# Local attention: row sums behind the row maxima, the token shift in four parts, the output product behind the weighted values

## The chip, the cores and the metric

The kernel runs on one core of one Trainium2 chip. The metric is the device time of one execution in microseconds (us). Three executions of the kernel before took 1742.20, 1739.64 and 1736.16 us, a median of 1739.64.

## The reference

The program computes four blocks with residuals over 16 x 256 tokens of 128 features: a linear attention with two decays, a mixture of eight experts, a retention layer, and a two-layer local attention with a gated feed-forward network. The change is in the attention half of the last block, which runs twice (DEPTH is 2). Its core, for each layer:

```python
h = shift_token(x)                  # features 64..127 come from the token before
qkv = h @ wqkv                      # 8 heads of 64
q = l2norm(q) * qs                  # row sums of squares, then 1/sqrt
k = l2norm(k) * ksc
q, k = rotary_xpos(q, k)
...
sim = jnp.einsum('bhwid,bhwjd->bhwij', bq, bk)      # windows of 64, one back
sim = jnp.where(mask, -jnp.finfo(sim.dtype).max, sim)
attn = jax.nn.softmax(sim, axis=-1)                 # subtracts the row maximum
out = jnp.einsum('bhwij,bhwjd->bhwid', attn, bv)
...
x = x + o @ wo
```

## The kernel before, in words

`local_layer(k, l, shared)` does one layer. The 4096 tokens are 8 chunks of 512 columns (two sequences of 256); a chunk has 4 tiles of 128 tokens (`t`), and 8 pairs of units (`p`: a pair is two heads of one sequence). Every engine runs the same software pipeline, written out by hand: `steps` calls `step` ten times. In step g the chunk g is projected (`project`), the scores and weighted values of chunk g-1 are made (`attend`), and what is left of chunk g-2 is finished (`finish`). Step 0 of a layer only projects, step 1 projects and attends, steps 2 to 7 do all three (they are the body of a loop of two steps), steps 8 and 9 drain. A step has 8 blocks (`blk`). Tile t belongs to blocks 2t and 2t+1. Semaphores join the engines; on each engine the order is the order of the code.

In an even block PE (TensorE) runs `project_qk` (six matmuls, L1582, into the PSUM banks BA and BB); ACT squares both banks (`squares`, L1733); DVE multiplies both with the rotation table (`rotate`, L1836), sums the squares by head (`lengths`, L1843 and the clip L1846); ACT turns the sums into 1/sqrt (`norms`, L1738 and L1741); POOL adds the two rotated halves (L1557) and multiplies with the norms (L1564). In an odd block PE runs `project_v` (L1591) once the first half of the rotation has read bank BA, ACT copies it (`keep_values`, L1762), and PE transposes the tile before (`turn`, L1608), which ACT copies twice (`keep_rows`, L1749 and L1756). The next `project_qk` waits for the L1749 copies.

Beside that, every block of a full step carries attention work on pairs, each stage a block or more behind the last: `maxima_scores` on PE (L1622, L1626), `maxima` on DVE (L1855, L1857: the masked row maxima, `nm`), `scores` and `less_maxima` on PE (L1643 to L1658), `weights` on ACT (L1773, exp), `weighted_values` on PE (L1670, L1671), `denominators` on ACT (L1779, L1781), `normalise` on DVE (L1866). The maxima use two PSUM banks for every pair, so `maxima_scores` of a block waits until DVE has read the maxima of the block before:

```python
need(pe, max_r, NU * c + 2 * p)
```

In blocks 2 and 6 the maxima of half a chunk are also transposed by PE (L1677) and copied by ACT (`maxima_rows`, L1767), and `less_maxima` waits for that copy. In block 4 of a finishing step PE runs `output` (L1687, eight matmul records), which needs bank BB and therefore the whole rotation of the tile; DVE adds it in block 5 (`add_output`, L1873). The token shift of the next chunk (`shift_chunk`, L1819 to L1823: the rounded value `hs_hi` and the rest `hs_lo`, halves of 64 partitions each) runs on DVE at the end of block 6, and the first `project_qk` of the next step waits for it (`shifted`).

Of the kernel before, what the change touches and what calls it, by code (L numbers as in the profile page):

```python
# [15 lines left out]
P = 128  # L16
# [1426 lines left out]
def later(a):  # L1443

    return a.rearrange("p (s t) -> p s t", t=SEQ)[:, :, 1:SEQ]
# [19 lines left out]
def need(eng, sem, value):  # L1465

    if not isinstance(value, int) or value > 0:
        eng.wait_ge(sem, value)


def local_layer(k, l, shared):
# [5 lines left out]
    with ExitStack() as big:  # L1477
# [4 lines left out]
        with ExitStack() as ctx:  # L1482
# [86 lines left out]
            def _(pe):  # L1569
# [120 lines left out]
                def step(g, par, project, attend, finish):  # L1690
                    now = (g, par, project, attend, finish)
                    for blk in range(2 * NTILE):
# [17 lines left out]
                            less_maxima(sc[0], sc[2])  # L1710
                        if blk % 2 and rows:
                            turn(rows[0], rows[2], project, g - 2 if finish and blk == 5 else None)
                        if finish and blk == 4:
                            output(g - 2, par, NTILE * g + t if project else None)
                        if mx and blk in (2, 6):
                            maxima_scores(*mx)
                        if av:
                            weighted_values(*av)

                steps(pe, step)  # L1720

            @block.scalar
            def _(act):
# [59 lines left out]
                def step(g, par, project, attend, finish):  # L1783
                    now = (g, par, project, attend, finish)
                    for blk in range(2 * NTILE):
                        t = blk // 2
                        if project and blk % 2 == 0:
                            squares(g, t)
                        if project and blk % 2:
                            keep_values(g, par, t)  # L1790
                        rows = turned_at(g, par, project, attend, blk)
                        if attend and blk in (2, 6):
                            maxima_rows(g - 1, blk // 4)
                        dn = staged(*now, blk, 4)
                        if dn:
                            denominators(dn[0], dn[2])
                        sc = staged(*now, blk, 2)
                        if sc:
                            weights(sc[0], sc[2])
                        if blk % 2 and rows:  # L1800
                            keep_rows(*rows)
                        if project and blk % 2 == 0:
                            norms(g, t)

                steps(act, step)
# [2 lines left out]
            def _(dve):  # L1808
# [3 lines left out]
                        nc.vector.tensor_scalar(t[:], k.H[:, T:T + CH], 1.0, None, ALU.mult).then_inc(made, 1)  # L1812
                dve.wait_ge(made, 5 * L)

                def shift_chunk(g, par):

                    hi, lo = hs[0][par], hs[1][par]
                    early_rows, late_rows = shifted_views(k, here(g))
                    nc.vector.tensor_scalar(hi[0:DH, :], early_rows, 1.0, None, ALU.mult)  # L1819
                    nc.vector.tensor_scalar(later(hi[DH:P, :]), late_rows, 1.0, None, ALU.mult).then_inc(hs_hi, 1)  # L1820
                    dve.wait_ge(hs_hi, g + 1 + l)
                    nc.vector.tensor_tensor(lo[0:DH, :], early_rows, hi[0:DH, :].bitcast(F32), ALU.subtract)
                    nc.vector.tensor_tensor(later(lo[DH:P, :]), late_rows, later(hi[DH:P, :]).bitcast(F32),  # L1823
                                            ALU.subtract).then_inc(shifted, 1)

                shift_chunk(G0, 0)
                dve.wait_ge(zeroed, 4 * L)

                def rotate(g, t):
# [54 lines left out]
                def step(g, par, project, attend, finish):  # L1884
                    now = (g, par, project, attend, finish)
                    for blk in range(2 * NTILE):
                        t = blk // 2
                        if project and blk % 2 == 0:
                            rotate(g, t)
                            lengths(g, t)  # L1890
                        if finish and blk == 5:
                            add_output(g - 2)
                        mx = maxima_at(g, project, attend, blk)
# [4 lines left out]
                        nr = staged(*now, blk, 4)  # L1898
                        if nr:
                            normalise(*nr)  # L1900
                        if project and blk == 6:
                            need(dve, v_mm, NTILE * g)
                            shift_chunk(g + 1, 1 - par)

                steps(dve, step)

# [239 lines left out]
```

## Time and profile before

| what | value |
|---|---|
| runs of the kernel before, us | 1742.20, 1739.64, 1736.16 |
| the profiled execution's own time, us | 1738.83 |
| its span, us | 1737.0 |
| busy in the span | PE 1400.4 (81%), DVE 1153.1 (66%), ACT 939.0 (54%), POOL 620.9 (36%) |
| the two attention stages, us from the span's start | 740.6 to about 1124, 1239.7 to about 1625 |

The span is the profiled execution from its first instruction to its last; the 1.8 us around it belong to the time too. A group line reads: line, engine, operation, names of what is written and read, number of instructions, then busy time and mean duration in ns, then the idle time of the engine just before them and what ended most of it. PE counts matmuls, PEld weight loads.

### The profile page before, as it was taken

Reading aid. Unit: us, or ns where it says so; the run is one execution under the profiler, and the core shown is the slowest. Engines: PE = TensorE matmul, PEld = TensorE weight load, DVE = VectorE, ACT = ScalarE, POOL = GpSimd, SP = SyncE. Lnnn points to the kernel's source line nnn. Section 1 sums busy time; section 2 is a strip of 40 time slices with the busy share of each in tenths; the row PEclk is TensorE's granted clock in tenths of the full one; section 3 lists DMA queues with packets and bytes.
Section 4 is the critical chain, followed back from the end, with each engine's and each line's share of the span. In section 5 each row is a group of like instructions: output and inputs, shape, how many; then the busy total and the mean of one; then the engine's idle time right before and its main releaser. Section 6 shows DMA issues by size and latency. Waiting matters only on the chain. (4 is left out here: it accounts for less than half of the span.)

```text
span 1737.0 us, 24232 instructions
## 1 busy us (share of the span) xinstructions
PE 1400.4 (81%) x7076; PEld 889.5 (51%) x7076; DVE 1153.1 (66%) x2595; ACT 939.0 (54%) x1756; POOL 620.9 (36%) x536
## 2 busy tenths in 40 slices
PE   6799998656399667668888988988578889889887
PEld 3233333444388532146666666733356666666433
DVE  1499999387288654457777777544568777776343
ACT  5523332443266335636777777644257777776543
POOL 0244343357366630344444434020344434442000
PEclk9899999678699979859999999999669999999998
DMA  4500000311212130000000000000000000000001
GB/s 132 195 1 1 0 1 1 87 48 50 71 60 81 37 133 0 19 1 1 2 2 0 1 1 1 1 26 0 19 1 2 2 1 0 1 0 1 1 0 49
DMA packets 35305, 44.53 MB, mean 26 GB/s; under 512 B 5652, under 2 KB 25137, under 8 KB 35200
## 3 DMA queue, kind: packets, MB, share of 16 engines
q1 hardware_dynamic: 30592, 34.91, 6.4%
q0 software_dynamic: 4608, 8.47, 1.5%
q8 instruction: 36, 0.59, 0.1%
q14 instruction: 69, 0.57, 0.1%
HBM read 23.28 MB, written 21.12 MB: 26 GB/s over the span
## 5 line engine op out<-in xcount | busy, mean ns | idle before, releaser
L1557 POOL TENSOR_TENSOR R<-R 128x512 f32<-128x512 f32 x128 | 159.3, 1265 | 392.9 <-DVE R L1836 392.9
L1836 DVE TENSOR_TENSOR R<-bank,tab 128x1024 f32<-128x1024 f32 x128 | 151.7, 1220 | 137.9 <-ACT sq L1733 132.7
L1564 POOL TENSOR_TENSOR R<-R,rn 128x512 f32<-128x512 f32 x128 | 133.7, 1065 | 12.1 <-issue 10.0
L1670 PE MATMUL bank<-PT,VA 128*128 128x192 f32 x512 | 131.4, 339 | 0.0
L1866 DVE TENSOR_TENSOR OT<-bank,rd 64x256 f32<-64x256 f32 x256 | 106.2, 415 | 18.2 <-ACT rd L1781 16.5
L1733 ACT ACTIVATE sq<-bank 128x512 f32<-128x512 f32 x128 | 76.2, 597 | 64.6 <-PE bank L1582 58.6
L1773 ACT ACTIVATE PT<-bank 128x320 f32<-128x320 f32 x256 | 98.3, 435 | 16.0 <-PE bank L1658 11.2
L1195 POOL DMA_INDIRECT expert_rows<-Yt,xin x80 | 82.5, 1031 | 67.7 <-DVE Yt L1168 49.7
L1582 PE MATMUL bank<-wqkv_hi,hs_hi 128*128 128x512 f32 x128 | 63.1, 493 | 49.3 <-DVE hs_lo L1823 39.3
L1855 DVE CUSTOM_DVE_ANT_0 masked<-bank,mask_q 128x128 bf16<-128x128 f32 x256 | 73.7, 288 | 42.0 <-PE bank L1626 31.4
L617 DVE TENSOR_TENSOR_SCAN S<-beta,U 128x512 f32<-128x512 f32 x64 | 100.0, 1583 | 0.0
L1671 PE MATMUL bank<-PT,VA 128*128 128x128 f32 x512 | 99.0, 275 | 0.0
L1671 PEld LDWEIGHTS bank<-PT,VA 128*128 128x128 f32 x512 | 91.3, 192 | 0.0
L1622 PE MATMUL bank<-QKr 64*128 64x128 f32 x256 | 42.9, 332 | 59.6 <-DVE nm L1857 59.6
L1857 DVE CUSTOM_DVE_ANT_0 masked<-bank,mask_q 128x192 bf16<-128x192 f32 x256 | 90.2, 352 | 0.2 <-issue 0.2
L1779 ACT ACTIVATE rd<-bank 64x512 f32<-64x512 f32 x128 | 76.0, 593 | 16.7 <-PE bank L1671 14.1
L1670 PEld LDWEIGHTS bank<-PT,VA 128*128 128x128 f32 x512 | 79.5, 193 | 9.5 <-issue 6.7
L1781 ACT ACTIVATE rd<-rd 64x512 f32<-64x512 f32 x128 | 80.7, 631 | 4.1
L1608 PE MATMUL bank<-ident,R 128*128 128x128 f32 x512 | 76.2, 296 | 6.0 <-ACT VA L1762 5.7
L1749 ACT ACTIVATE QK<-bank 128x512 f32<-128x512 f32 x128 | 71.0, 608 | 11.9 <-PE bank L1608 11.8
L1843 DVE TENSOR_REDUCE ss<-sq 128x16 f32<-128x1024 f32 x64 | 77.3, 1208 | 0.0
L888 POOL DMA_INDIRECT expert_slots<-tok_rows,dst x64 | 64.1, 1001 | 33.6 <-issue 18.0
(311 smaller groups left out, 3805.6 us busy)
## 6 DMA issues: line engine op xcount, KB each, us to landing
expert_slots<-empty SPq DMA_DIRECT2D x8, 650.0 KB, 6.5
xin<-expert_slots SPq DMA_DIRECT2D x8, 650.0 KB, 5.1
expert_rows<-empty SPq DMA_DIRECT2D x8, 512.0 KB, 6.7
pair_rows<-expert_rows SPq DMA_DIRECT2D x16, 256.0 KB, 3.8
expert_raw<-w1e_dram SPq DMA_DIRECT2D x9, 256.0 KB, 2.9
expert_raw<-w2e_dram SPq DMA_DIRECT2D x9, 256.0 KB, 2.9
tok<-x_dram SPq DMA_DIRECT2D x8, 256.0 KB, 4.8
out_dram<-tok_out SPq DMA_DIRECT2D x8, 256.0 KB, 2.5
```

What stands on the lines that cost most here:

```text
L617: nc.vector.tensor_tensor_scan(S[i][:], beta[i % 2][:, chunk(c)], U[i // 2][:], 0.0, ALU.mult, ALU.add).then_inc(s_scan, 1)
L1195: nc.gpsimd.indirect_dma_start(k.ys[:, :], bass.IndirectOffsetOnAxis(ap=ids, axis=0), Yt[:, s % 3, t, :], None, bounds_check=2 * T - 1, oo ...
L1557: nc.gpsimd.tensor_tensor(halves[:, :, 0, :, z, :], halves[:, :, 0, :, z, :], halves[:, :, 1, :, 1 - z, :], ALU.add).then_inc(summed, 1)
L1564: nc.gpsimd.tensor_tensor(x, x, scale.to_broadcast([P, HEADS, DH]), ALU.mult).then_inc(normed, 1)
L1670: nc.tensor.matmul(bank[:, o:o + KW], VA[par][:, 2 * s, h, :], pt[:, 0:KW], start=True, stop=True)
L1671: nc.tensor.matmul(bank[:, o + P:o + SEQ], VA[par][:, 2 * s + 1, h, :], pt[:, KW:KW + P], start=False, stop=True, skip_group_check=True).t ...
L1773: nc.scalar.activation(PT[:, u % 4, :], ps[BT + u % 2][:, 0:KW + P], ACT.Exp, scale=QK_SCALE).then_inc(pt_r, 1)
L1781: nc.scalar.activation(rd[:, p % 2, :], rd[:, p % 2, :], ACT.Exp, scale=-1.0).then_inc(rd_r, 1)
L1836: nc.vector.tensor_tensor(R[:, i, qk, :, :].rearrange("p c (h d) -> p c h d", d=DH), x, y.to_broadcast([P, 2, HEADS, DH]), ALU.mult).then_ ...
L1843: nc.vector.tensor_reduce(ss[:, i, :], sq[:].rearrange("p q (h d) -> p (q h) d", d=DH), AX.X, ALU.add).then_inc(sums_r, 1)
L1857: nc.vector.tensor_tensor_reduce(masked[:, v % 2, KW:2 * KW], bank[:, KW:2 * KW], mask[:, KW:2 * KW], -1.0, FAR, ALU.add, ALU.min, nm[:, 2 ...
L1866: m = nc.vector.tensor_tensor(OT[par][i * DH:(i + 1) * DH, b, s * SEQ:(s + 1) * SEQ], ps[BO + p % 2][0:DH, i * SEQ:(i + 1) * SEQ], rd[:, p ...
```

## The change

Nothing is computed in another way, and no instruction is added or removed: instructions move on three engines.

- DVE: `lengths` moves from just behind `rotate` to the end of the even block, behind `maxima` and `normalise`. `shift_chunk` is cut into its four instructions, and one of them ends each odd block (part 0 in block 1, part 3 in block 7).
- ACT: in odd blocks `denominators` stands first, ahead of `keep_values`; `norms` moves from the end of the even block to the end of the odd block, behind `keep_rows`.
- PE: in block 4 `output` runs behind `weighted_values`.

```diff
                         if blk % 2 and rows:
                             turn(rows[0], rows[2], project, g - 2 if finish and blk == 5 else None)
-                        if finish and blk == 4:
-                            output(g - 2, par, NTILE * g + t if project else None)
                         if mx and blk in (2, 6):
                             maxima_scores(*mx)
                         if av:
                             weighted_values(*av)
+                        if finish and blk == 4:
+                            output(g - 2, par, NTILE * g + t if project else None)
...
                         if project and blk % 2 == 0:
                             squares(g, t)
+                        dn = staged(*now, blk, 4)
+                        if dn and blk % 2:
+                            denominators(dn[0], dn[2])
                         if project and blk % 2:
                             keep_values(g, par, t)
                         rows = turned_at(g, par, project, attend, blk)
                         if attend and blk in (2, 6):
                             maxima_rows(g - 1, blk // 4)
-                        dn = staged(*now, blk, 4)
-                        if dn:
+                        if dn and blk % 2 == 0:
                             denominators(dn[0], dn[2])
                         sc = staged(*now, blk, 2)
                         if sc:
                             weights(sc[0], sc[2])
                         if blk % 2 and rows:
                             keep_rows(*rows)
-                        if project and blk % 2 == 0:
+                        if project and blk % 2:
                             norms(g, t)
...
-                def shift_chunk(g, par):
+                def shift_part(g, par, part):
...
-                    nc.vector.tensor_scalar(hi[0:DH, :], early_rows, 1.0, None, ALU.mult)
-                    nc.vector.tensor_scalar(later(hi[DH:P, :]), late_rows, 1.0, None, ALU.mult).then_inc(hs_hi, 1)
-                    dve.wait_ge(hs_hi, g + 1 + l)
-                    nc.vector.tensor_tensor(lo[0:DH, :], early_rows, hi[0:DH, :].bitcast(F32), ALU.subtract)
-                    nc.vector.tensor_tensor(later(lo[DH:P, :]), late_rows, later(hi[DH:P, :]).bitcast(F32),
-                                            ALU.subtract).then_inc(shifted, 1)
...
+                    if part == 0:
+                        need(dve, v_mm, NTILE * (g - 1))
+                        nc.vector.tensor_scalar(hi[0:DH, :], early_rows, 1.0, None, ALU.mult)
+                    elif part == 1:
+                        nc.vector.tensor_scalar(later(hi[DH:P, :]), late_rows, 1.0, None, ALU.mult).then_inc(hs_hi, 1)
+                    elif part == 2:
+                        dve.wait_ge(hs_hi, g + 1 + l)
+                        nc.vector.tensor_tensor(lo[0:DH, :], early_rows, hi[0:DH, :].bitcast(F32), ALU.subtract)
+                    else:
+                        nc.vector.tensor_tensor(later(lo[DH:P, :]), late_rows, later(hi[DH:P, :]).bitcast(F32),
+                                                ALU.subtract).then_inc(shifted, 1)
...
                         if project and blk % 2 == 0:
                             rotate(g, t)
-                            lengths(g, t)
                         if finish and blk == 5:
                             add_output(g - 2)
                         mx = maxima_at(g, project, attend, blk)
...
                         if nr:
                             normalise(*nr)
-                        if project and blk == 6:
-                            need(dve, v_mm, NTILE * g)
-                            shift_chunk(g + 1, 1 - par)
+                        if project and blk % 2 == 0:
+                            lengths(g, t)
+                        if project and blk % 2:
+                            shift_part(g + 1, 1 - par, t)
```

DVE in an even block of step 1, before; each `masked,nm` row with the `nm` row behind it is one of the maxima of a pair.

```order
L1836 TENSOR_TENSOR R<-bank,tab 128x1024 x2
L1843 TENSOR_REDUCE ss<-sq 128x16
L1846 TENSOR_SCALAR ss<-ss 128x16
L1855 ISA masked,nm<-bank,mask_q 128x128
L1855 ISA nm 128x1
L1857 ISA masked,nm<-bank,mask_q 128x192
L1857 ISA nm 128x1
L1855 ISA masked,nm<-bank,mask_q 128x128
L1855 ISA nm 128x1
L1857 ISA masked,nm<-bank,mask_q 128x192
L1857 ISA nm 128x1
```

The same place now (lines are numbered anew: L1844 is the rotation, L1863 and L1865 the maxima, L1851 and L1854 the row sums and their clip).

```order
L1844 TENSOR_TENSOR R<-bank,tab 128x1024 x2
L1863 ISA masked,nm<-bank,mask_q 128x128
L1863 ISA nm 128x1
L1865 ISA masked,nm<-bank,mask_q 128x192
L1865 ISA nm 128x1
L1863 ISA masked,nm<-bank,mask_q 128x128
L1863 ISA nm 128x1
L1865 ISA masked,nm<-bank,mask_q 128x192
L1865 ISA nm 128x1
L1851 TENSOR_REDUCE ss<-sq 128x16
L1854 TENSOR_SCALAR ss<-ss 128x16
```

The maxima follow the rotation directly, and the two instructions of the row sums stand behind them.

ACT in blocks 4 and 5 of step 1, before; `sq` is the squares, `rd` the denominators, `PT` the weights, `ss` and `rn` the norms, `VA` the values, `QK` and `QKr` the kept rows.

```order
L1733 ACTIVATE sq<-bank 128x512 x2
L1779 ACTIVATE rd<-bank 64x512
L1781 ACTIVATE rd<-rd 64x512
L1773 ACTIVATE PT<-bank 128x320 x2
L1738 ACTIVATE ss<-ss 128x16
L1741 ACTIVATE rn<-ss,lnb 128x16
L1762 ACTIVATE VA_1<-bank 128x8x64
L1779 ACTIVATE rd<-bank 64x512
L1781 ACTIVATE rd<-rd 64x512
L1773 ACTIVATE PT<-bank 128x320 x2
L1749 ACTIVATE QK_1<-bank 128x4x128 x2
L1756 ACTIVATE QKr<-QK_1 128x4x128 x2
```

And now:

```order
L1733 ACTIVATE sq<-bank 128x512 x2
L1779 ACTIVATE rd<-bank 64x512
L1781 ACTIVATE rd<-rd 64x512
L1773 ACTIVATE PT<-bank 128x320 x2
L1779 ACTIVATE rd<-bank 64x512
L1781 ACTIVATE rd<-rd 64x512
L1762 ACTIVATE VA_1<-bank 128x8x64
L1773 ACTIVATE PT<-bank 128x320 x2
L1749 ACTIVATE QK_1<-bank 128x4x128 x2
L1756 ACTIVATE QKr<-QK_1 128x4x128 x2
L1738 ACTIVATE ss<-ss 128x16
L1741 ACTIVATE rn<-ss,lnb 128x16
```

The norms stand between the kept rows and the squares of the next tile; the second pair of `rd` is ahead of `VA`.

PE at the end of block 4 of a full step, as a piece of the difference (`OT` goes through the output product, `PT` through the weighted values; L1589 belongs to the `project_v` of block 5).

```order
 L1658 MATMUL bank<-mT_0,sel 128x128
+L1670 MATMUL bank<-PT,VA_1 128x192
+L1671 MATMUL bank<-PT,VA_1 128x128
+L1670 MATMUL bank<-PT,VA_1 128x192
+L1671 MATMUL bank<-PT,VA_1 128x128
 L1681 REGISTER_ALU
 L1687 MATMUL bank<-OT_0,wo_0 128x512 x4
-L1670 MATMUL bank<-PT,VA_1 128x192
-L1671 MATMUL bank<-PT,VA_1 128x128
-L1670 MATMUL bank<-PT,VA_1 128x192
-L1671 MATMUL bank<-PT,VA_1 128x128
 L1589 REGISTER_ALU
```

The output product changes places with the weighted values of the block.

## Rows read from the trace of the kernel before

**Rows 1.** Windows of step 0 and of full steps in the first layer; columns named above.
```profile
core 0: us, PE busy (x) PEld busy (x) DVE busy (x) ACT busy (x) POOL busy (x), PEclk, DMA share, GB/s
740.60:777.70 37.10, 23.91 (x69) 15.24 (x69) 20.11 (x29) 15.04 (x32) 18.25 (x16) 0.59 0.00 1
821.00:1078.00 257.00, 226.49 (x1731) 173.97 (x1730) 194.72 (x602) 189.19 (x400) 105.19 (x92) 0.99 0.00 1
```

**Rows 2.** Waits of the whole span: us in total, times, longest.
```profile
ACT ss L1738 <- DVE ss L1846: 89.0, 64, 2.8
...
PE bank L1622 <- DVE nm L1857: 59.6, 48, 2.7
...
PE bank L1582 <- DVE hs_lo L1823: 39.3, 16, 14.5
```

**Rows 3.** Windows of the four tiles of one full step, columns as rows 1.
```profile
1453.50:1463.30 9.80, 8.59 (x73) 6.99 (x74) 9.58 (x36) 7.24 (x16) 4.55 (x4) 1.00 0.00 0
1463.30:1473.10 9.80, 9.02 (x78) 7.22 (x76) 7.50 (x25) 8.34 (x19) 4.54 (x4) 1.00 0.00 0
1473.10:1486.40 13.30, 12.41 (x83) 8.62 (x82) 8.38 (x27) 8.24 (x18) 4.54 (x4) 1.00 0.00 1
1486.40:1497.30 10.90, 9.21 (x74) 7.24 (x74) 8.82 (x19) 9.40 (x21) 4.72 (x4) 1.00 0.00 0
```

**Rows 4.** Timeline of PE over that step: start, us, instruction, idle before it.
```profile
1453.54 0.50 PE L1582 MATMUL bank<-wqkv_hi,hs_hi 128*128 128x512 f32 x1 [0.83 <-DVE hs_lo L1823]
...
1460.15 0.33 PE L1622 MATMUL bank<-QKr 64*128 64x128 f32 x2 [1.16 <-DVE nm L1857]
...
1465.98 0.23 PE L1656 MATMUL bank<-mT,sel 128*128 128x128 bf16 x1
...
1466.76 0.59 PE L1670 MATMUL bank<-PT,VA 128*128 128x192 f32 x2
...
1467.88 0.48 PE L1591 MATMUL bank<-wqkv_hi,hs_hi 128*128 128x512 f32 x1
...
1469.90 0.33 PE L1622 MATMUL bank<-QKr 64*128 64x128 f32 x2 [0.78 <-DVE nm L1857]
...
1477.22 3.70 PE L1687 MATMUL bank<-OT,wo 128*128 128x512 f32 x8 [0.83 <-DVE R L1836]
...
1493.17 0.33 PE L1622 MATMUL bank<-QKr 64*128 64x128 f32 x2 [0.90 <-DVE nm L1857]
```

**Rows 5.** Timeline of ACT, start of its second tile.
```profile
1463.08 1.17 ACT L1756 ACTIVATE QKr<-QK 128x512 fp32r<-128x512 f32 x2
1464.29 1.30 ACT L1733 ACTIVATE sq<-bank 128x512 f32<-128x512 f32 x2
1465.48 0.27 ACT L1767 ACTIVATE mT<-bank 128x128 bf16<-128x128 bf16 x1
```

**Rows 6.** Timeline of DVE, same tile.
```profile
1465.01 2.35 DVE L1836 TENSOR_TENSOR R<-bank,tab 128x1024 f32<-128x1024 f32 x2 [1.55 <-ACT sq L1733]
1467.28 1.21 DVE L1843 TENSOR_REDUCE ss<-sq 128x16 f32<-128x1024 f32 x1
1468.53 0.23 DVE L1846 TENSOR_SCALAR ss<-ss 128x16 f32<-128x16 f32 x1
...
1469.76 0.84 DVE L1866 TENSOR_TENSOR OT<-bank,rd 64x256 f32<-64x256 f32 x2
```

**Rows 7.** The shift: source view of L1819 (min/median/max), timelines of POOL and DVE.
```profile
L1819 DVE TENSOR_SCALAR hs_hi<-H x18: 418/722/880, 738.2 to 1583.1; 64x512 fp32r x12, 64x512 fp32r<-64x512 f32 x6
...
1493.31 2.23 POOL L1564 TENSOR_TENSOR R<-R,rn 128x512 f32<-128x512 f32 x2 [0.21 <-issue]
...
1494.65 1.17 DVE L1820 TENSOR_SCALAR hs_hi<-H 64x510 fp32r x1
```

**Rows 8.** Timelines of ACT and PE in step 0 of layer 0.
```profile
754.37 0.21 ACT L1738 ACTIVATE ss<-ss 128x16 f32<-128x16 f32 x1 [2.73 <-DVE ss L1846]
...
755.46 1.11 PE L1608 MATMUL bank<-ident,R 128*128 128x128 f32 x4 [1.29 <-ACT VA L1762]
```

**Rows 9.** Timeline of PE at the start of step 8, layer 0.
```profile
1090.48 0.33 PE L1622 MATMUL bank<-QKr 64*128 64x128 f32 x2 [1.54 <-DVE nm L1857]
```

More of the change, by code:

```diff
@@ L1813, in _ @@
                 dve.wait_ge(made, 5 * L)
-                def shift_chunk(g, par):
+                def shift_part(g, par, part):
                     hi, lo = hs[0][par], hs[1][par]
                     early_rows, late_rows = shifted_views(k, here(g))
-                    nc.vector.tensor_scalar(hi[0:DH, :], early_rows, 1.0, None, ALU.mult)
-                    nc.vector.tensor_scalar(later(hi[DH:P, :]), late_rows, 1.0, None, ALU.mult).then_inc(hs_hi, 1)
-                    dve.wait_ge(hs_hi, g + 1 + l)
-                    nc.vector.tensor_tensor(lo[0:DH, :], early_rows, hi[0:DH, :].bitcast(F32), ALU.subtract)
-                    nc.vector.tensor_tensor(later(lo[DH:P, :]), late_rows, later(hi[DH:P, :]).bitcast(F32),
-                                            ALU.subtract).then_inc(shifted, 1)
-                shift_chunk(G0, 0)
+                    if part == 0:
[9 more added lines that the diff above has]
+                                                ALU.subtract).then_inc(shifted, 1)
+                for part in range(4):
+                    shift_part(G0, 0, part)
                 dve.wait_ge(zeroed, 4 * L)
```

## The prediction

> **What bounds the kernel now.** First I read the windows of the two attention stages, since the change touches nothing else. In full steps PE is busy 226.5 of 257.0 us, DVE 194.7 and ACT 189.2, at a granted clock of 0.99 [rows 1]: PE is near its limit, and what can be won is its idle time. In step 0 PE is busy only 23.9 of 37.1 us, at a clock of 0.59 of full speed. Then I read the waits [rows 2]: PE waits 59.6 us in 48 waits, ahead of the matmuls for the maxima (L1622), for DVE's maxima of the block before; 39.3 us in 16 waits for the shifted tokens, of which one alone, at a layer's start, is 14.5. ACT waits 89.0 us in all 64 tiles for the clipped row sums. Last I read one full step on PE tile by tile [rows 3, 4]. Its tiles take 9.8, 9.8, 13.3 and 10.9, 43.8 us together. The waits are 1.16 in tile 0, 0.78 in tile 1, 0.83 before the output product in tile 2, and in tile 3 0.90 and, as the next projection starts, 0.83 as at the head of this one: 4.50 us a step that PE could gain at most. There are 12 such steps, 6 in each layer.
>
> **Row sums behind the maxima.** L1843 and L1846 take 1.21 + 0.23 us with small gaps, 1.44 to 1.5 together [rows 6]. They stand between the rotation and the maxima, for which PE waits in each odd block. Moved back, the maxima end 1.45 us earlier relative to the rotation's start. That covers the waits of 1.16, 0.78 and 0.90 if the rotation starts when it does now. All other terms ask whether it does, and what is late next.
>
> **Norms last on ACT.** In the kernel before, ACT stands idle in each even block until the clip is done. Now norms come after the kept rows, when the sums are long ready, so that wait goes. But the kept rows end at 1464.25 and the squares of the next tile start at 1464.29 [rows 5]: ACT is already late there, since PE's projection is ready by then. The two norms (0.21 for the first [rows 8]; with the second, slightly longer, and their gap about 0.55, an estimate) now sit in this place, on the path projection, squares, rotation. I take 0.55 us later for the squares and so for the rotation in tiles 1, 2 and 3 of a full step; least 0 (if denominators placed first let ACT reach the weights earlier; in tile 2 it does win about 0.35), at most 0.7. In blocks 2 and 6 the transposed maxima are copied behind the squares (L1767, ending 1465.75), and L1656, which waits for it, starts at 1465.98 [rows 4, 5]: 0.2 us of slack, so 0.35 to 0.5 turns into a new PE wait there in block 2.
>
> POOL's products come later with the norms, but their user, the transposition, is a block and a half further on; I cost that at nothing. If that cover failed, the transposes would wait up to POOL's 2.2 us [rows 7].
>
> **Full steps, tile by tile.**
> - Tile 0: the rotation follows a project_qk that itself waited for the shift, so ACT is free and the delay is hidden. The whole 1.16 goes. Saving 1.16 (0.8 to 1.16).
> - Tile 1: the 0.78 goes, but the new wait ahead of L1656 costs up to 0.5; behind it the maxima are in time. Saving 0.25. Bounds: 0.78, and a loss of 0.4 if part 0 of the shift is slow (below).
> - Tile 2: the output product waits 0.83 for the rotation. The weighted values, 1.12 us of PE work (1466.76 to 1467.88), now run inside that wait; against it stands the later rotation, 0.55, so that a wait of 0.2 to 0.5 is left. Saving 0.4 (0 to 0.83). DVE's add comes behind the product, as before, and DVE idles there.
> - Tile 3: the shift leaves block 6 (0.73 + 1.17 + 0.68 + 0.69, 3.3 us), but its last part, 0.69, stands in block 7 behind that block's maxima and normalise, and these behind the row sums. DVE's path, start to start [rows 6]: rotation 2.27, row sums 1.5, maxima 1.0, normalise 0.87. Before, from the rotation to the end of the shift: 2.27 + 1.5 + 1.0 + 0.87 + 3.35 = 9.0. Now: 2.27 + 1.0 + 0.87 + 1.5 + 1.0 + 0.87 + 0.69 = 8.2. Of the 0.8 won the later rotation takes about 0.4 back (0.55 less what the denominators win in tile 2). So this tile is still closed by the shift: the 0.90 wait goes, and the wait for hs_lo grows from 0.83 to about 1.3. Saving 0.4 (from -0.5 to 0.9).
>
> Together 1.16 + 0.25 + 0.4 + 0.4 = 2.21 a step, times 12 = 26.5 us.
>
> **The shift's parts.** The same instruction L1819 takes 0.418 at the least and 0.722 in the median; L1820 took 1.17 while POOL's second product ran [rows 7]. Part 0 now ends block 1: by the path above it starts some 1.2 us after the next projection (1.7 to the rotation, 8.0 behind it with the split of the maxima, less the tile's 8.6), and POOL's products of the tile, which wait for the norms, some 0.6 later. So it takes 0.42 or up to 1.17. The first is hidden by the wait for the squares, the second, if the order turns, delays the rotation of tile 1 by about 0.6: that is the loss bound of tile 1. I take the first; the other would take 0.65 x 12 = 8 us from the sum. The Trainium skill ("SBUF — State Buffer", section "SBUF: two separate sides") says that DVE in a two-port mode and GpSimd hold their shared port exclusively for a whole instruction; this trace agrees, as the 1.17 above beside 0.418 alone shows. By that rule spreading the parts puts some of them beside POOL's work and some not, and the slow part 0 would be the case of the sentence before.
>
> **Step 0, twice.** There ACT's values copy waits behind the norms, which wait 2.73 us for the sums; PE's second group of transposes waits 1.29 for that copy [rows 8], then the next projection for the kept rows. Now the copy runs as soon as project_v is done, about 1.4 earlier. I take 1.4 for tile 0, 1.2 each for tiles 1 and 2 (PE's first transposes fill the rest), and 1.4 for tile 3, where the row sums leave both the maxima's path and the shift's. 5.2 a layer, 10.4 in all (5 to 16: at the upper end a denser PE also gets its full clock sooner than at the 0.59 of now).
>
> **Step 1, twice.** Waits of up to 2.7 us for the maxima shrink by 1.1 in tiles 0 and 1 and 0.5 in tile 2, nothing in tile 3: 2.75 a layer, 5.5 in all (2 to 8).
>
> **End of step 7, twice.** No projection follows there, so the shift is only a burden: in the kernel before it held up the maxima of block 7 and PE waited 1.54 at the next maxima [rows 9], after 1.26 in the tile. Both go: 2.8 a layer, 5.6 in all (3 to 5.6). The drain in steps 8 and 9 has no projection and keeps its order but for the output product: 0.
>
> **Sum.** 26.5 + 10.4 + 5.5 + 5.6 = 48.0. The profiled execution took 1738.8 us (span 1737.0 and 1.8 around it), the median of the runs 1739.6, so the two differ by less than 1. I forecast 1739.6 - 48.0 = 1692 us.
>
> **Rivals.**
> 1. *Full steps give nothing* (chance 0.19). The waits turn up one for one at L1656, at L1687 and as a longer hs_lo wait, since ACT's squares and with them DVE's rotation are late in every tile. For it: ACT has no idle before the squares in three tiles of four [rows 5]. Against it: in tile 0 the squares are not held. Time: 1739.6 less the 21.5 of steps 0, 1 and 7 = 1718.
> 2. *More than the sum* (0.10). Denominators first bring ACT forward enough to hide the norms, tiles 1 to 3 lose 0.78, 0.83 and 0.9; with tile 0 that is 3.67 x 12 = 44, plus 21.5: 1674.
> 3. *Slower* (0.09). The loop closes through the last part of the shift. Place: project_qk of tile 0, waiting for hs_lo. Maxima, normalise and row sums all stand before part 3, and the rotation that starts the chain is itself later by the norms. If both of block 7's items wait for PE as well, the wait grows from 0.83 to over 5 us, a step loses 2.5 net; 12 x 2.5 = 30, less some 15 won in steps 0, 1 and 7: 1739.6 + 15 = 1755. It decides from where the hs_lo wait exceeds about 4.5 us; the chain above gives 1.3. Against it: DVE has 9.5 us of idle in a 43.8 us step (34.3 busy, the sum of [rows 3]).
> 4. *No change* (0.10): within 0.3%, which is about what a measurement of this kernel can tell from no change. PE's gaps are refilled everywhere, steps 0 and 1 included, as when PE loses in clock what it gains in waits. 1739.6.
>
> **How the numbers follow.** My forecast's own case has 0.52. Faster by over 0.3% (below 1734) are the forecast, rivals 1 and 2: 0.81; same 0.10; slower 0.09. The range reaches from 1680 (60 us: the upper bounds of most terms) to 1722 (rival 1, with some of its gains missing); it leaves out the last two rivals and part of the second.
>
> **What the profile of the changed kernel would show.** Right: the wait of PE's L1622 for the maxima falls from 59.6 us to under 15; ACT's wait for the clipped sums (89.0) vanishes; the hs_lo wait in full steps is 1 to 2 us each instead of 0.83; a new wait of some 0.4 at less_maxima (L1656) in block 2; the output product's wait is 0.2 to 0.5; a full step takes about 41.6 us instead of 43.8; step 0 takes 32 us instead of 37. Wrong: squares that start no later than now after the projection (then the step is shorter, near 40.5), or a step not shorter than 43.5 (rival 1), or an hs_lo wait beyond 3 us.

## The result and the profile after

The changed kernel took 1657.07 us in the median of four runs (1655.81 to 1662.76), against 1740.14 before: a ratio of 0.9524, with a 95% interval of 0.9503 to 0.9544. It is faster by 83 us, where I forecast 48 and a range down to 1680. The sign was right, and so was the main mechanism (the row sums no longer stand between the rotation and the maxima that PE waits for); the size was not.

The page of the profile after, its span and busy times; then the windows of step 0 and of full steps in layer 0, with the columns of [rows 1].

```profile
span 1656.2 us, 24233 instructions
PE 1384.4 (84%) x7076; PEld 879.5 (53%) x7076; DVE 1131.6 (68%) x2595; ACT 929.6 (56%) x1756; POOL 621.3 (38%) x536
```
```profile
739.90:767.60 27.70, 17.75 (x68) 11.13 (x68) 20.45 (x36) 14.59 (x31) 16.93 (x14) 0.81 0.00 1
804.90:1038.00 233.10, 224.30 (x1732) 172.38 (x1733) 187.28 (x602) 184.98 (x398) 104.96 (x92) 1.00 0.00 1
```

In full steps PE is now busy 96% of the time (224.3 of 233.1), before 88%. The waits of the whole span, as in [rows 2], lines numbered anew:

```profile
PE bank L1582 <- DVE hs_lo L1830: 44.9, 16, 14.5
...
PE bank L1622 <- DVE nm L1865: 4.2, 6, 1.1
...
PEld bank L1656 <- ACT mT L1767: 1.9, 6, 0.4
```

PE's wait for the maxima fell from 59.6 us to 4.2, ACT's 89.0 us for the clipped sums are gone from the list, and the wait for the shift grew from 39.3 to 44.9. The four tiles of the full step that was read before, now 1386.60 to 1426.75 (it answers to [rows 3]):

```profile
1386.60:1395.10 8.50, 8.50 (x73) 6.96 (x74) 6.60 (x23) 6.83 (x14) 4.56 (x4) 1.00 0.00 0
1395.10:1404.00 8.90, 8.90 (x77) 7.17 (x75) 8.12 (x28) 8.09 (x19) 4.57 (x4) 1.00 0.00 0
1404.00:1416.30 12.30, 12.23 (x83) 8.59 (x82) 9.56 (x31) 8.03 (x18) 4.54 (x4) 1.00 0.00 1
1416.30:1426.70 10.40, 9.18 (x77) 7.27 (x75) 8.48 (x26) 9.55 (x22) 4.55 (x4) 1.00 0.00 1
```

PE is busy without a gap in tiles 0 and 1, and but for 0.07 us in tile 2. Its timeline shows what is left; it answers to [rows 4]:

```profile
1386.60 0.50 PE L1582 MATMUL bank<-wqkv_hi,hs_hi 128*128 128x512 f32 x1 [1.26 <-DVE hs_lo L1830]
...
1397.79 0.23 PE L1656 MATMUL bank<-mT,sel 128*128 128x128 bf16 x1
...
1408.57 3.70 PE L1687 MATMUL bank<-OT,wo 128*128 128x512 f32 x8
...
1426.75 0.50 PE L1582 MATMUL bank<-wqkv_hi,hs_hi 128*128 128x512 f32 x1 [1.27 <-DVE hs_lo L1830]
```

Beside these 0.07 us there is one wait a step, 1.26 us for the last part of the shift. The following table cuts both profiled executions at the first matmul of the projections (L1582), and sets the difference beside the forecast's terms.

| stretch | before, us | after, us | gained | forecast |
|---|---|---|---|---|
| step 0, layers 0 and 1 | 37.1, 37.0 | 27.8, 30.9 | 15.4 | 10.4 |
| step 1 | 41.5, 41.8 | 37.3, 36.6 | 9.4 | 5.5 |
| steps 2 to 6 | 226.1, 224.2 | 204.1, 201.4 | 44.9 | 22.1 |
| step 7 to the next layer or the end | 194.5, 194.3 | 189.2, 189.1 | 10.4 | 10.0 |
| before the first projection | 740.6 | 739.9 | 0.8 | 0 |

Most of what I missed is in steps 2 to 6. A regular step fell from 43.86 to 40.16, tile by tile from 9.77, 9.79, 13.37, 10.94 to 8.53, 8.93, 12.30, 10.40. That is 3.70 us a step against my 2.21. Before, two steps of each layer were not regular: steps 4 and 6, each behind a jump of the loop (its body is two steps, so its jumps stand ahead of steps 4 and 6), took 47.6 and 45.7 us in layer 0, 47.2 and 45.4 in layer 1.

### The profile page after: what moved, and what is told of

The parts are those of the page before. It is cut to its first block and busy times, and to the rows that moved or that the text cites. A ratio compares the mean times of both kernels' runs of the same rounds, so it can differ in the third digit from the quotient of the medians.

```text
span 1656.2 us, 24233 instructions
## 1 busy us (share of the span) xinstructions
PE 1384.4 (84%) x7076; PEld 879.5 (53%) x7076; DVE 1131.6 (68%) x2595; ACT 929.6 (56%) x1756; POOL 621.3 (38%) x536
## 5 line engine op out<-in xcount | busy, mean ns | idle before, releaser
L1844 DVE TENSOR_TENSOR R<-bank,tab 128x1024 f32<-128x1024 f32 x128 | 151.5, 1221 | 93.9 <-ACT sq L1733 90.7
L1582 PE MATMUL bank<-wqkv_hi,hs_hi 128*128 128x512 f32 x128 | 61.3, 479 | 51.0 <-DVE hs_lo L1830 44.9
L1733 ACT ACTIVATE sq<-bank 128x512 f32<-128x512 f32 x128 | 71.0, 589 | 50.4 <-PE bank L1582 48.8
L1865 DVE CUSTOM_DVE_ANT_0 masked<-bank,mask_q 128x192 bf16<-128x192 f32 x256 | 90.4, 353 | 0.0
L1863 DVE CUSTOM_DVE_ANT_0 masked<-bank,mask_q 128x128 bf16<-128x128 f32 x256 | 73.5, 287 | 22.1 <-PE bank L1626 13.6
L1851 DVE TENSOR_REDUCE ss<-sq 128x16 f32<-128x1024 f32 x64 | 78.0, 1219 | 1.6
L1756 ACT ACTIVATE QKr<-QK 128x512 fp32r<-128x512 f32 x128 | 74.8, 649 | 0.0
L2010 DVE SCALAR_TENSOR_TENSOR Uf<-bank,vec,Gg 128x512 f32<-128x512 f32 (+1 forms) x48 | 36.0, 750 | 52.0 <-PE bank L1962 52.0
```

The costliest lines, as they stand in the source:

```text
L1844: nc.vector.tensor_tensor(R[:, i, qk, :, :].rearrange("p c (h d) -> p c h d", d=DH), x, y.to_broadcast([P, 2, HEADS, DH]), ALU.mult).then_ ...
L1851: nc.vector.tensor_reduce(ss[:, i, :], sq[:].rearrange("p q (h d) -> p (q h) d", d=DH), AX.X, ALU.add).then_inc(sums_r, 1)
L1865: nc.vector.tensor_tensor_reduce(masked[:, v % 2, KW:2 * KW], bank[:, KW:2 * KW], mask[:, KW:2 * KW], -1.0, FAR, ALU.add, ALU.min, nm[:, 2 ...
```

## The experiments

Twelve kernels ran. A ratio is always to the kernel before, run beside it on the same chip; on two of the chips everything outside the attention took some 30 to 50 us longer, for before too, so between chips I compare ratios and the lengths of regular steps; tiles that an edit leaves alone agree on all chips to some 0.01 us (8.53, 8.93 and 10.40 in u_output as in the changed kernel). "A step" is a regular full step in layer 1, from projection to projection: 43.86 us before, 40.16 after.

**Taking one edit back from the changed kernel.**

u_sums:
```diff
                             rotate(g, t)
+                            lengths(g, t)
...
-                        if project and blk % 2 == 0:
-                            lengths(g, t)
```


> The changed kernel with the row sums back between rotation and maxima; all else as changed (1657 us). Theory A (the row sums on the maxima's path are the main term, and the norms' later squares add to it, since the rotation now starts 0.35 us later): PE's waits for nm return, about 1.1 us in tile 0 and 1.1 in tile 1 of a full step, nothing in tile 3 (the shift closes that tile, and the chain to it holds the row sums either way): 2.2 x 12 = 27 us, and 3 to 4 us a layer in steps 0 and 1: about 1690. Theory B (the moves on ACT are what counts and the row sums' place is second): 1657 to 1668.

Measured: ratio 0.9815 (0.9775 to 0.9854), a step 42.77 us: tiles 9.83, 10.15, 12.28, 10.51. Theory A holds for the regular step: tiles 0 and 1 lose 1.3 and 1.2, tile 2 nothing and tile 3 0.1. The time that it gave, 1690 or a ratio of 0.971, was some 18 us too low: the steps behind the jumps of layer 0 take 47.2 and 47.8 us again (the changed kernel's 41.5 and 41.7), and steps 0 take 32.4 in both layers instead of 27.8 and 30.9. Its waits:
```profile
PE bank L1622 <- DVE nm L1865: 62.3, 45, 3.0
```

u_shift:
```diff
-                        if project and blk % 2:
-                            shift_part(g + 1, 1 - par, t)
+                        if project and blk == 6:
+                            for part in range(4):
+                                shift_part(g + 1, 1 - par, part)
```


> The changed kernel with all four parts of the shift at the end of block 6. Theory A (the spread shortens DVE's chain in tile 3 by some 0.7 us, and leaves DVE free 1.5 us earlier at the end of a step, which hides its restart after the loop's jump): full steps +0.7 to 1.0 us, the two jumps of each layer +1.5 us each, the end of step 7 +1.5 us a layer: about +18 us, 1675. Theory B (the spread only moves work that is hidden anyway): within 4 us of 1657.

Measured: 0.9511 (0.9475 to 0.9547), which can't be told from the changed kernel's. My theory A missed: a regular step is 40.10 us, as with the spread. The whole shift in block 6, on DVE's timeline:
```profile
874.93 0.42 DVE L1823 TENSOR_SCALAR hs_hi<-H 64x512 fp32r x1
875.37 0.42 DVE L1825 TENSOR_SCALAR hs_hi<-H 64x510 fp32r x1
```
In the kernel before, its first two parts took 0.72 (median) and 1.17 [rows 7], when they met POOL's products. With the norms late on ACT they come clear of them and take 0.42 each (in the full steps of o_act too, below), so the shift takes some 2.25 us instead of 3.3. Behind the jumps steps grow to 41.0 to 41.3; the stretch of steps 2 to 6 of both layers is 405.5 us, as in the changed kernel. With ACT's edit in place the spread is worth nothing that can be measured; alone (o_shift, below) it is worth 0.8 a step.

u_norms:
```diff
-                        if project and blk % 2:
+                        if project and blk % 2 == 0:
                             norms(g, t)
```


> The changed kernel with the norms back at the end of the even block, while the row sums stay behind maxima and normalise. Theory A (ACT's queue then waits for sums that are ready only some 7.3 us after the projection, and values copy, denominators, weights and kept rows queue behind): tiles 0 and 1 of a full step +2 to 3 us each, tile 3 +1.5, so +6 us x 12 = 70 and some 10 in steps 0 and 1: about 1735, all of the gain given back. Theory B (norms last costs 0.35 us of later squares and saves an ACT wait that nobody needed, so taking it back is neutral): 1650 to 1662.

Measured: 1.0284 (1.0240 to 1.0329), slower than before, a step 47.8 us in layer 1 and 50.9 in layer 0. Theory A holds and was too mild. Its longest wait:
```profile
ACT ss L1738 <- DVE ss L1854: 182.2, 64, 3.9
```

u_output:
```diff
+                        if finish and blk == 4:
+                            output(g - 2, par, NTILE * g + t if project else None)
                         if mx and blk in (2, 6):
                             maxima_scores(*mx)
                         if av:
                             weighted_values(*av)
-                        if finish and blk == 4:
-                            output(g - 2, par, NTILE * g + t if project else None)
```


> The changed kernel with the output product back ahead of the weighted values in block 4. Theory A (the wait for the rotation, now 0.07 us, comes back as 0.83 + 0.35 = 1.1 to 1.2, in 12 steps): +13 us, 1670. Theory B (what the product waits for comes late anyway, and the time is given back at the next wait): within 4 us of 1657.

Measured: 0.9567 (0.9527 to 0.9607). The step is 41.25 us, all of it in tile 2 (13.39 against 12.30): +1.09 a step, theory A. The interval overlaps with the changed kernel's, so it is the step that shows it, not the time.

**One edit alone on the kernel before.**

o_sums (the lines that u_sums takes back, put in alone):
```diff
                             rotate(g, t)
-                            lengths(g, t)
...
+                        if project and blk % 2 == 0:
+                            lengths(g, t)
```


> The kernel before (1740 us) with only the row sums moved behind maxima and normalise. Theory A (the moves need each other: ACT's norms, still at the end of the even block, now wait for sums that come 3 us later, and everything behind them on ACT is late): slower, 1775 to 1800. Theory B (PE's wait for the maxima goes, 1.16 + 0.78 + 0.90 a step): about 1705.

Measured: 1.0264 (1.0228 to 1.0301), 1787.9 us against 1743.1, a step 47.9. Theory A. PE's wait for the maxima does go, and ACT's takes its place:
```profile
ACT ss L1738 <- DVE ss L1846: 188.8, 64, 4.0
...
PE bank L1622 <- DVE nm L1857: 9.5, 10, 1.3
```

o_act:
```diff
+                        dn = staged(*now, blk, 4)
+                        if dn and blk % 2:
+                            denominators(dn[0], dn[2])
                         if project and blk % 2:
                             keep_values(g, par, t)
...
-                        dn = staged(*now, blk, 4)
-                        if dn:
+                        if dn and blk % 2 == 0:
                             denominators(dn[0], dn[2])
...
-                        if project and blk % 2 == 0:
+                        if project and blk % 2:
                             norms(g, t)
```


> The kernel before with only ACT's moves (norms last, denominators first in odd blocks). Theory A: steps 0 gain about 5 us a layer since the values copy no longer waits for the norms, full steps lose 0 to 0.35 us a tile because squares come later while the waits for the maxima stay: 1725 to 1735. Theory B (ACT's wait for the clipped sums, 89 us in all, was on the path): below 1710.

Measured: 0.9913 (0.9886 to 0.9941), 1728.0 us. A step is 43.9, unchanged, but its tiles are not: 10.11, 10.15, 13.39 and 10.23. Tiles 0 and 1 lose some 0.35 each, and tile 3 wins 0.7: the shift's first two parts take 0.42 each there, clear of POOL's products, and the wait for hs_lo is gone. Neither theory said that. Steps 0 fell to 28.8 and 32.4 us, so ACT's moves alone bring 12.9 of the 15.4 us won there. Theory A. Behind the jumps of layer 0 steps take 47.2 and 48.8 us, not less than before.

o_shift:
```diff
-                        if project and blk == 6:
-                            need(dve, v_mm, NTILE * g)
-                            shift_chunk(g + 1, 1 - par)
+                        if project and blk % 2:
+                            shift_part(g + 1, 1 - par, t)
```


> The kernel before with only the shift spread. Theory A: tile 3 loses its 0.83 wait for hs_lo (the chain rotation, sums, maxima, normalise, maxima, normalise, part 3 is 1.8 + 8.2 = 10.0 against 10.95), 0.9 x 12 = 11; the steps behind the loop's jump (steps 4 and 6) lose their extra 1.4 to 1.7 us in DVE's rotation, which will start 1.7 us after the projection as in other steps and not 3.1 to 3.4 after it: 6; step 7's end 3: about 1720. Theory B (the rotation's late start behind the jump is not DVE's restart but something all engines pay): the rotation stays at 3.1 to 3.4 there, time 1726 to 1730.

Measured: 0.9883 (0.9850 to 0.9917), 1723.8 us. A step is 43.07, tile 3 10.15. In layer 1 the steps behind the jumps take 43.2 and 43.1 us, and the rotation starts 1.71 us after the projection there: theory A. In layer 0 they still take 44.9 and 47.5, and there ACT's squares are late too (2.4 to 2.7 us after the projection instead of 1.0), which neither theory said. (Before, they stood at 1.7 and 1.9 in these two steps.)

before_unrolled:
```diff
-                with eng.Fori(0, NCH // 2 - 1) as x:
+                for x in range(NCH // 2 - 1):
                     step(2 * x + (G0 + 2), 0, True, True, True)
                     step(2 * x + (G0 + 3), 1, True, True, True)
```


> The kernel before with the loop over steps 2 to 7 written out (no jump, the same instructions in the same order). Theory A (the steps behind a jump take 47.6, 45.7, 47.2 and 45.4 us instead of 43.9, because DVE restarts 1.4 to 1.7 us late, and in two of them PE's idle time drops its granted clock for 3.4 us): all steps about 43.9, -10 us, 1730. Theory B (the extra time has another cause, such as the clock alone, or straight code is fetched no faster): 1736 to 1745.

Measured: 0.9892 (0.9863 to 0.9921), 1723.7 us. All steps 2 to 6 take 43.5 to 43.8 us, none is longer than its neighbours: the jump is the cause of the irregular steps. The gain is 19 us in the medians instead of the 10 that I expected. The profiled spans differ by 14.9, of which steps 2 to 6 hold 14.6: 11.7 for the irregular steps (below), and 0.3 in each of the ten. The other 4 or so are not accounted for.

**The pair, the slack, and what is left.**

p_sums_act (the changed kernel with u_shift's and u_output's edits together; the second is not shown again):
```diff
-                        if project and blk % 2:
-                            shift_part(g + 1, 1 - par, t)
+                        if project and blk == 6:
+                            for part in range(4):
+                                shift_part(g + 1, 1 - par, part)
```


> Only the row sums' and ACT's moves; shift whole at the end of block 6, output product early. Alone, the sums cost 4.1 us a full step and ACT's moves 0. Theory A (the two belong together: late sums keep the maxima off PE's path only if the norms leave the even block): a full step of 41.2 us, as the changed kernel's 40.2 plus the 1.1 of the output product, ratio to before about 0.959, near 1668 against 1740. Theory B (all four edits are needed; the output product's wait and the shift close the loop otherwise): 43 us a step or more, above 1710.

Measured: 0.9625 (0.9576 to 0.9674), a step 41.21 us. Theory A: alone the sums cost 4.1 us a step and ACT's moves nothing, together they win 2.65. The ratio that I expected, 0.959, lies within the interval.

d_act:
```diff
                         if project and blk % 2:
                             norms(g, t)
+                        if project and attend and blk % 2:
+                            nc.scalar.activation(spare[:].rearrange("p (a b) -> p a b", a=NB),
+                                                 QK[rows[1]][:, 0:NB, rows[2] * P:(rows[2] + 1) * P], ACT.Copy)
```


> The changed kernel with one more ACT instruction of about 0.6 us between the norms and the next tile's squares (a copy of kept rows into a spare tile), in attending steps. Theory A (the norms took up the last slack there: the maxima's copy now ends 0.07 us before L1656 needs it, the output product waits 0.07, and the hs_lo chain has none): tiles 1, 2 and 3 each +0.55, so 1.65 x 12 = 20 us, a ratio to before of about 0.964. Theory B (ACT has slack there still, since the norms cost nothing to be seen): less than 5 us.

Measured: 0.9651 (0.9600 to 0.9702). The copy takes 0.614 us. The tiles are 8.54, 9.44, 12.81, 10.92: +0.01, +0.51, +0.51, +0.52, a step 41.71. Theory A, whose 0.55 a tile was 0.04 too much; its waits are the ones that I had forecast for the changed kernel itself (L1657 is less_maxima here, L1688 the output product):
```profile
PE bank L1657 <- ACT mT L1768: 11.4, 26, 0.5
...
PE bank L1688 <- DVE R L1848: 7.0, 12, 0.6
```

v_early:
```diff
-                        if project and blk % 2:
+                        if project and blk in (1, 3, 5):
                             shift_part(g + 1, 1 - par, t)
+                        if project and blk == 5:
+                            shift_part(g + 1, 1 - par, 3)
```


> The changed kernel with the shift's parts at the ends of blocks 1, 3, 5 and 5 (the last two together), none in block 7. Theory A (the 1.26 us wait for hs_lo is the last PE wait of a full step, and DVE is idle in block 5 behind the output product): tile 3 falls from 10.4 to about 9.1, a step from 40.2 to 38.9; with steps 0 and 1 some 17 us, less up to 5 behind the loop's jumps, where DVE's and ACT's restart is no longer hidden: 1642. Theory B (the norms' delay or DVE's last normalise takes the wait's place one for one): above 1652.

Measured: 0.9500 (0.9454 to 0.9545), which can't be told from the changed kernel's. A regular step is 38.71 us, tile 3 8.89: theory A on that point, but not in its time (1642, a ratio of 0.944). The steps behind jumps take 42.9, 43.0, 39.5 and 39.7 us: 4 us lost each in layer 0 and 10.3 in all, where I had allowed 5. ACT's timeline behind the first jump of layer 0:
```profile
930.60 0.31 ACT L1741 ACTIVATE rn<-ss,lnb 128x16 f32<-128x16 f32 x1
933.34 1.08 ACT L1733 ACTIVATE sq<-bank 128x512 f32<-128x512 f32 x2 [2.43 <-issue]
```
ACT stands still for 2.43 us, with nothing to wait for but its own queue, and that starts only when the norms are done. In the changed kernel ACT is idle for 2.37 us at this place, and its squares start 2.3 us after the projection, since the projection itself waits 1.26 us for the shift; here, where it doesn't, they start 3.9 us after it.

v_early_unrolled (both edits):
```diff
-                with eng.Fori(0, NCH // 2 - 1) as x:
+                for x in range(NCH // 2 - 1):
```


> The same as v_early with the loop over steps 2 to 7 written out. Theory A (behind a jump DVE and ACT restart 1.4 to 2.4 us late, and nothing else differs): 2 to 6 us faster than v_early, about 1638. Theory B (the jump costs nothing once PE does not wait for DVE there): as v_early within 2 us.

Measured: 0.9421 (0.9377 to 0.9464), 1682.6 us beside 1786.8 for the kernel before and 1698.6 for v_early on that chip. It beats both kernels; all steps 2 to 6 take 38.4 to 38.6 us. That is 16 us less than v_early, where I expected 2 to 6. In the profiled executions steps 2 to 6 hold 13.5 us of it; 3.2 more are in step 0 of layer 1 (29.9 and 26.7), which stands ahead of the loop and had PE's full clock sooner this time, so they are no proof against the jump.

## Why the prediction was wrong

**Row sums behind the maxima: right.** The waits of 1.16, 0.78 and 0.90 went, and u_sums brings back 1.22, 1.14 and 1.25, the last in place of the wait for hs_lo. What I did not see is how much this edit depends on the norms: alone it makes the kernel 2.6% slower.

**Norms last on ACT: the step that failed.** I took the squares 0.55 us later, and said "0.35 to 0.5 turns into a new PE wait there in block 2". The timeline of ACT after, which answers to [rows 5]:

```profile
1394.89 1.17 ACT L1756 ACTIVATE QKr<-QK 128x512 fp32r<-128x512 f32 x2
1395.93 0.23 ACT L1738 ACTIVATE ss<-ss 128x16 f32<-128x16 f32 x1
1396.28 0.31 ACT L1741 ACTIVATE rn<-ss,lnb 128x16 f32<-128x16 f32 x1
1396.49 1.06 ACT L1733 ACTIVATE sq<-bank 128x512 f32<-128x512 f32 x2
1397.45 0.28 ACT L1767 ACTIVATE mT<-bank 128x128 bf16<-128x128 bf16 x1
```

The projection started at 1395.12, so the squares start 1.37 after it, where they started 0.98 after it before: 0.39 later, not 0.55, since the norms overlap with their neighbours. I had also read that ACT "is already late there". It was not: in tile 0 of that step ACT had stood waiting for the projection, and its squares started 1.00 after it, so the 0.98 of tile 1 is when the first bank is ready. And the two squares take 1.06 us instead of the 1.30 of [rows 5], because the second had been waiting for PE's second bank and now finds it ready. So the maxima's copy ends 2.61 us after the projection instead of 2.44, and L1656 starts 2.67 after it, as it did: no wait. The delay of one instruction was carried through as if everything behind it had been running back to back. In tile 2 the output product waits 0.07 us, where I had 0.2 to 0.5. That tile won 0.3 more than its wait before the output product lost. In o_act, with ACT's moves alone, the same wait is 1.21 instead of 0.83, and yet the tile takes 13.39, as before:

```profile
1468.27 1.12 PE L1687 MATMUL bank<-OT,wo 128*128 128x512 f32 x2 [1.21 <-DVE R L1838]
```

So ACT's moves win at the tile's end what the later rotation costs in its middle. There the weights of the next projection waited for the kept rows in the kernel before, and no longer do in o_act and in the changed kernel. Waits of before in the window 1484:1487:

```profile
PEld bank L1582 <- ACT QK L1749: 0.3, 1, 0.3
```

Whether the norms' leaving or the earlier denominators did it, no run separates. Tiles 1 and 2 won 0.86 and 1.07 instead of 0.25 and 0.4. Over 12 steps these two terms are 15 us. d_act shows that the mechanism is there: 0.6 us more in that place costs 0.51 in each of the three tiles. Only the size was off, and that the delay just fitted into the slack is luck that I did not foresee: I had named squares no later than before as the sign of a step near 40.5, and the step is 40.16 with squares that are later.

**Tile 3: right.** I gave it 0.4 us and a wait for hs_lo of 1.3; it won 0.54, and the wait is 1.26. The parts of the shift before that are all fast, since part 0 runs ahead of POOL's products:

```profile
1396.22 0.42 DVE L1823 TENSOR_SCALAR hs_hi<-H 64x512 fp32r x1
```

**The loop's jumps: missed altogether.** I multiplied one regular step by twelve and never looked at whether all steps are regular. Steps 2 to 6 of both layers, the ones behind a jump above all, took 11.7 us more before than ten regular steps, and take 3.8 more after: 7.9 us gained that no term had. DVE behind the first jump of layer 1, before:

```profile
1407.17 0.84 DVE L1866 TENSOR_TENSOR OT<-bank,rd 64x256 f32<-64x256 f32 x2
1409.71 2.36 DVE L1836 TENSOR_TENSOR R<-bank,tab 128x1024 f32<-128x1024 f32 x2 [1.70 <-issue]
```

and after:

```profile
1345.45 0.69 DVE L1830 TENSOR_TENSOR hs_lo<-H,hs_hi 64x510 fp32r<-64x510 f32 x1
1348.02 2.36 DVE L1844 TENSOR_TENSOR R<-bank,tab 128x1024 f32<-128x1024 f32 x2 [1.88 <-ACT sq L1733]
```

Before, DVE ended its step 1.7 us after PE had begun the next projection (1406.32), so its 1.7 us of restart delayed the rotation. Now the shift is the last thing in DVE's step, PE's projection waits for it, and the restart passes while projection and squares run. In layer 1 o_shift shows this alone, and before_unrolled shows that the jump is the cause of the long steps.

But the spread is not what won most of the 7.9 us. The table has what steps 2 to 6 took beyond five regular steps of the same kernel.

| kernel | layer 0, us | layer 1, us |
|---|---|---|
| before | 6.8 | 4.9 |
| changed | 3.3 | 0.6 |
| u_shift (spread taken back) | 2.5 | 2.0 |
| u_sums (row sums taken back) | 9.8 | 1.3 |
| o_shift (spread alone) | 6.3 | 0.3 |

In layer 1 either edit brings most of it; in layer 0 the spread alone brings almost nothing, and without the row sums' move the jumps cost more than before. In u_shift the rotation behind the first jump of layer 1 starts 3.11 us after the projection, almost as late as before (3.39). But PE's wait for the maxima behind it, 2.39 us before, is now

```profile
1379.61 0.33 PE L1622 MATMUL bank<-QKr 64*128 64x128 f32 x2 [0.87 <-DVE nm L1865]
```

since the row sums no longer stand between the two. So the 1.45 us that I had counted for regular steps pay a second time behind the jumps.

With the long wait went a drop of PE's granted clock to the lower level (1.2 GHz) for 3.4 us in step 4 of both layers, 9.8 and 9.5 us into the step and soon behind a PE wait of 2.39 us. PE's timeline of before, and the window behind the wait:

```profile
1414.63 0.33 PE L1622 MATMUL bank<-QKr 64*128 64x128 f32 x2 [2.39 <-DVE nm L1857]
```
```profile
1414.60:1420.00 5.40, 5.37 (x37) 5.15 (x37) 3.05 (x14) 4.22 (x8) 2.06 (x3) 0.68 0.00 0
```

It cost about 1.9 us each time (tile 0 took 13.1 us in these two steps and 11.2 in the steps behind the other jumps, where a wait of 2.38 us was followed by no drop; what decides between them no run tells). In the changed kernel's full steps PE has no such wait, and the clock stays at 1.00.

**Step 0: right in layer 1, too small in layer 0.** Layer 1 gained 6.1 for my 5.2. Layer 0 gained 9.3, as tiles 2 and 3 took 6.2 and 8.6 us instead of 7.8 and 9.2: there PE's clock rose to its full level from the second tile on, and the stage's granted clock is 0.81, where it was 0.59 before and still is 0.59 in layer 1. o_act shows the same split (28.8 and 32.4). I had named this as the upper end; in which layer it comes is not explained.

**Step 1: too small.** Its tiles won 1.4, 1.0, 1.1 and 0.7 in layer 0, where I took 1.1, 1.1, 0.5 and 0. The last two may be the same error as above, the late rotation carried through without slack; my terms for this step had no rows behind them that could tell.

**Step 7's end: too large, and hidden in a right sum.** The stretch won 10.4 for my 10.0, but that is luck. Its first three tiles won 6.3 us in both layers together, where I had 3.6; the rest of step 7 and the drain won 4.1, where I had 6.4. The waits of 1.26 (in layer 1 only 0.91) and 1.54 are gone, but a new one stands in step 8:

```profile
1051.26 0.45 PE L1632 MATMUL bank<-mask_k,identb 128*128 128x320 bf16 x2 [0.57 <-ACT PT L1773]
```

**The rivals.** Rival 2 (norms hidden) came nearest: its 3.67 us a step stand beside 3.70 measured, though tile 3 won less and tile 2 more than it said. Even that gave 1674, since it too knew nothing of the jumps and took my steps 0 and 1. Rival 1's refilling at L1656 and L1687 did not happen, and rival 3's hs_lo wait stayed at 1.26.

Missed in sum: the ten steps 2 to 6 taken as regular 15, their jumps 8, step 0 5, step 1 4, rest 1: 33 us, which with the forecast's 48 makes the 81 between the two spans.

Still open: why ACT's restart behind a jump shows in layer 0 (2.4 us) and hardly in layer 1, and why the kernel with only the norms taken back is 3 us a step slower in layer 0 than in layer 1. No run here tells.

## What to carry to other kernels

A delay put into a chain has to be followed with the waits of each instruction behind it: what had been waiting for something else absorbs it. Two moves of a hand-written order can be worth nothing or less alone and a lot together, so price the pair where one moves a producer that the other's consumer waits for. Before a period is multiplied by its count, list all periods: the irregular ones, here those behind a loop's jump, held 11.7 us beside a forecast of 48.

## What the hardware showed

- Behind a loop's jump DVE stood still for 1.70 us (kernel before) and ACT for 2.43 (v_early), both with nothing to wait for but their own queue. Whether it costs depends on what each engine does last in the body: it is free where the engine then has to wait for another anyway. With the loop written out, steps 2 to 6 of both layers took 14.6 us less in the kernel before and 13.5 less in v_early (profiled executions).
- A `tensor_scalar` of 64x512 from SBUF to SBUF took 0.42 us where POOL stood still, and 0.72 in the median beside POOL's products; the one of 64x510 behind it took 0.42 and 1.17.
